# Feed-forward on Trainium2: four token tiles a group, weights kept once, and the x rows held until the output

## The reference

```python
x = x + _L0_attn_ref(_layernorm(x), ...)
x = x + 0.5 * _L0_ffn_ref(_layernorm(x), ...)   # top-2 of 8 experts, gelu(gate) * up, down
x = x + 0.5 * _L1_ffn_ref(_layernorm(x), ...)   # below
x = x + _L1_attn_ref(_layernorm(x), ...)
x = x + 0.5 * _L1_ffn_ref(_layernorm(x), ...)

def _L1_ffn_ref(x, gate_w, up_w, down_w, gate_s, up_s, down_s):
    g = jnp.einsum('th,ih->ti', xf, gate_w) * gate_s      # 512 -> 1408
    u = jnp.einsum('th,ih->ti', xf, up_w) * up_s
    hdn = jax.nn.silu(g) * u
    out = jnp.einsum('ti,hi->th', hdn, down_w) * down_s   # 1408 -> 512
```

## Time and profile before

| | |
|---|---|
| time, median of 3 runs | 4873.7 us (4868.59 to 4876.05) |
| span of the profiled execution | 4868.5 us; its own time is taken as the nearest of the runs, 4868.59 us |
| TensorE busy | 4669.5 us, 96% |
| VectorE, ScalarE, GpSimd busy | 60%, 46%, 48% |
| mean granted TensorE clock | 0.975 of full |
| transfers | 593.49 MB, mean 122 GB/s |

### The profile page before, as it was taken

The page is one execution under the profiler, slowest core; times in us unless marked ns, Lnnn a source line. Parts: engine busy times, 40 slices in busy tenths (PEclk is TensorE's granted clock), DMA queues, the critical chain, the costliest instruction groups (busy, mean ns, idle before and its releaser), DMA issues. The chain is left out here.

```text
span 4868.5 us, 89120 instructions
## 1 busy us (share of the span) xinstructions
PE 4669.5 (96%) x30652; PEld 3639.6 (75%) x30653; DVE 2927.7 (60%) x5637; ACT 2238.0 (46%) x4551; POOL 2328.8 (48%) x1768
## 2 busy tenths in 40 slices
PE   6999996999999999999998799999899999999999
PEld 4788885666666666666656588887899987689999
DVE  6222225789999999999965522222655548774444
ACT  4222223466666666666662322222544335453333
POOL 1545433178888888888880335451411116430000
PEclk8999998899999999999999899999999999999999
DMA  7233226657777777777765623332522322251110
GB/s 220 80 93 100 91 85 228 238 109 147 147 147 147 147 147 147 147 147 147 147 126 181 188 90 97 94 98 66 195 92 92 95 86 61 80 185 51 53 53 32
DMA packets 253209, 593.49 MB, mean 122 GB/s; under 512 B 31616, under 2 KB 85888, under 8 KB 228352
## 3 DMA queue, kind: packets, MB, share of 16 engines
q0 software_dynamic: 62064, 317.23, 29.0%
q1 hardware_dynamic: 190736, 271.21, 17.0%
HBM read 262.22 MB, written 121.11 MB: 79 GB/s over the span
## 5 line engine op out<-in xcount | busy, mean ns | idle before, releaser
L1464 POOL TENSOR_TENSOR attend_pairs<-attend_pt 128x1024 f32<-128x1024 f32 x512 | 1257.6, 2476 | 198.6 <-ACT attend_pt L1429 197.9
L1477 DVE TENSOR_REDUCE attend_mx<-attend_am_ps 128x1 f32<-128x512 f32 x2048 | 1251.8, 679 | 123.9 <-PE attend_am_ps L1337 120.6
L1429 ACT ACTIVATE attend_pt<-attend_sc_ps 128x512 f32<-128x512 f32 x2048 | 1039.9, 617 | 283.9 <-PE attend_sc_ps L1325 283.6
L1337 PE MATMUL attend_am_ps<-attention_kst,attend_qst 96*128 96x512 f32 x2048 | 859.3, 425 | 9.2 <-DMA attend_qst<-q_parts 9.1
L1325 PE MATMUL attend_sc_ps<-attend_qst,attention_kst 98*128 98x512 f32 x2048 | 816.3, 400 | 1.5 <-ACT attend_pt L1429 1.3
L1337 PEld LDWEIGHTS attend_am_ps<-attention_kst,attend_qst 96*128 96x128 f32 x2048 | 393.1, 192 | 239.7 <-DVE attend_mx L1477 123.0
L727 DVE TENSOR_TENSOR expert_ac<-expert_gu_ps,expert_gl 128x512 f32<-128x512 f32 x142 | 98.3, 692 | 666.9 <-ACT expert_gl L687 666.9
L1351 PE MATMUL attend_pv_ps<-attend_pt,attention_v 128*32 128x256 f32 x8192 | 493.6, 381 | 0.0
L1325 PEld LDWEIGHTS attend_sc_ps<-attend_qst,attention_kst 98*128 98x128 f32 x2048 | 389.8, 191 | 86.9 <-ACT attend_pt L1429 11.7
L1351 PEld LDWEIGHTS attend_pv_ps<-attend_pt,attention_v 128*32 128x32 f32 x8192 | 246.3, 110 | 211.5 <-ACT attend_pt L1429 45.9
L1832 ACT ACTIVATE ffn_sg<-ffn_gu_ps,ffn_gs 128x256 f32<-128x256 f32 x352 | 167.1, 475 | 506.9 <-PE ffn_gu_ps L1753 506.9
(11 more groups left out here) (347 smaller groups left out, 9114.9 us busy)
## 6 DMA issues: line engine op xcount, KB each, us to landing
attend_pairs<-attend_pairs POOLq DMA_DIRECT2D x189, 1024.0 KB, 7.4
weights_raw<-experts_dram POOLq DMA_DIRECT2D x76, 512.0 KB, 4.2
ys<-expert_ob SPq DMA_DIRECT2D x142, 256.0 KB, 2.3
attend_qst<-q_parts SPq DMA_DIRECT2D x192, 128.0 KB, 3.9
yn<-route_yb SPq DMA_DIRECT2D x64, 256.0 KB, 4.0
ffn_xb<-x SPq DMA_DIRECT2D x64, 256.0 KB, 2.8
ffn_rb<-x SPq DMA_DIRECT2D x64, 256.0 KB, 3.0
keyvalue_xb<-x SPq DMA_DIRECT2D x64, 256.0 KB, 2.8
```

The costliest lines, as they stand in the source:

```text
L1337: pe.matmul(am[:, bank, :], qst[0:KROWS, n % 2, h * HALF + hd, :], kst[0:KROWS, o:o + 4 * P], start=True, stop=True).then_inc(am_rdy, 1)
L1429: act.activation(pt[:, u % RING, g * 4 * P:(g + 1) * 4 * P], sc[:, s % SBANKS, :], ACT.Exp, scale=HD ** -0.5).then_inc(p_rdy, 1)
L1464: pool.tensor_tensor(pairs[:, slot(half, j), :], pt[:, 2 * p % RING, :], pt[:, (2 * p + 1) % RING, :], ALU.add).then_inc(pair_rdy, 1)
L1477: dve.tensor_reduce(mx[:, hh, block:block + 1], am[:, am_slot["max", a] % MBANKS, :], AX.X, ALU.max).then_inc(mx_rdy, 1)
```

## The change

- Groups of four tiles, with one of two tiles at either end: 9 groups in place of 16. Gate and up move 512 columns a matmul. The down projection stays as it was, tile by tile. `y_hi` and `y_lo` have one buffer in place of two; the next group's first two tiles are turned after the first tile's down projection, the other two in the middle of the second tile's.
- The weights are kept once: they are loaded straight into an fp32r buffer, with no split on any engine, and every group multiplies two products (`y_hi` and `y_lo` by the weight). If the flag says that low parts exist, the same operands are multiplied as plain float32 instead.
- The test moves into the second expert stage: in every second of its steps SyncE loads a piece of the weights and copies it to a scratch tensor in memory, ScalarE rounds the piece, VectorE compares and keeps the maximum. A reduction near the stage's end gives `low_seen`. ffn0 turns it into the flag at its very start; ffn1 uses the same flag.
- The x rows stay in `xb` (eight tiles) until the output; neither the joined x rows nor a second read of x goes through memory.
- In ffn0 all gathers are issued by GpSimd without casts between them. Statistics of the next group's tiles stand at blocks 1, 3, 5 and 7 of a group.

The diff, cut to its core:

```diff
 # expert_stage, only where tested
+                if tested and k == 0 and not last:                       # sync
+                    sp.wait_ge(ever_rdy, i + 1)
+                    sp.dma_start(raw_c[:], ffn_w[:, bass.ds(i, 1), :].rearrange("p a d -> p (a d)")).then_inc(c_in, 16)
+                    sp.dma_start(ffn_kept[:, bass.ds(i, 1), :], ffn_w[:, bass.ds(i, 1), :]).then_inc(c_kept, 16)
                 sp.wait_ge(ob_rdy, j + 1)
...
                     out(j - 1, k, i)                                      # scalar
+                    if tested and k == 0:
+                        act.wait_ge(c_in, i * 16 + 16)
+                        act.activation(hi_c[:], raw_c[:], ACT.Copy).then_inc(chi_rdy, 1)
...
                     x_part(j + 1, k)                                      # vector
+                    if tested and k == 1:
+                        dve.wait_ge(chi_rdy, i + 1)
+                        dve.tensor_tensor(differs[:], raw_c[:], hi_c[:].bitcast(F32), ALU.not_equal).then_inc(differs_rdy, 1)
+                        dve.wait_ge(differs_rdy, i + 1)
+                        dve.tensor_tensor(ever[:], ever[:], differs[:], ALU.max).then_inc(ever_rdy, 1)
 # ffn_stage
-GF = 2
+GF = 4
+FIRST = 2
+GROUPS = [(0, FIRST)] + [(t, GF) for t in range(FIRST, NT - GF + 1, GF)] + [(NT - FIRST, FIRST)]
...
+            def up(g, m, width, exact):
+                k = m % 2
+                pe.wait_ge(h_rdy, g * IC + max(m + 1, 2))
+                for q, done in enumerate((g_rdy, u_rdy)):
                     for c in range(DC):
+                        for n, y in enumerate((y_hi, y_lo)):
+                            a, b = w[:, 2 * m + q, c * P:(c + 1) * P], y[:, c, 0:width]
+                            if not exact:
+                                a, b = a.bitcast(F32), b.bitcast(F32)
+                            ins = pe.matmul(gu[:, k, q, 0:width], a, b, start=(c == 0 and n == 0), stop=(c == DC - 1 and n == 1))
+                    ins.then_inc(done, 1)
...
+            def step(g, first, n, following, exact):
+                pe.wait_ge(lo_rdy, first + n)
                 for m in range(IC):
+                    if isinstance(g, int) and g == 0:
+                        pe.wait_ge(gu_in[m], 16)
+                    up(g, m, n * P, exact)
+                after = [(first + n + j, (FIRST + j) % NY) for j in range(following)]
+                down(g, first, 0, exact)
+                for tile, slot in after[0:2]:
+                    turn(tile, slot)
+                down(g, first + 1, 1, exact, after[2:4])
+                for j in range(2, n):
+                    down(g, first + j, j, exact)
...
             warm(pe, const, tr[:, 0, 0:P], 50 if joined else 34)
+            if low_seen is not None:
+                pe.wait_ge(cmp_rdy, 1)
+                pe.matmul(gu[0:1, 1, 0, 0:1], const["ones"][:, 0:1], low_seen[:], start=True, stop=True).then_inc(cmp_rdy, 1)
+                pe.wait_ge(flag_rdy, 1)
...
+            if low_seen is not None:                                      # vector, ahead of stats(0)
+                dve.tensor_scalar(low_seen[:], low_seen[:], 0.0, None, ALU.not_equal).then_inc(cmp_rdy, 1)
+                dve.wait_ge(cmp_rdy, 2)
+                dve.tensor_scalar(flag[:], gu[0:1, 1, 0, 0:1], 1.0, None, ALU.min).then_inc(flag_rdy, 1)
+            for t in tiles(0):
+                stats(t)
+                moments(t)
+            for t in tiles(0):
+                scales([t])
+                normalise(t)
+            for t in tiles(0):
+                low(t)
...
+                for t in following:                                       # vector, at a group's end
+                    normalise(t)
+                for t in following[0:2]:
+                    low(t)
...
+                output(GROUPS[g][0])
+                for t in following[2:4]:
+                    low(t)
+                for t in list(tiles(g))[1:]:
+                    output(t)
```

More of the change, by code:

```diff
@@ L1671, in _, with tiles, columns, both @@
+        def tiles(g):
+            return range(GROUPS[g][0], sum(GROUPS[g])) if g < NG else range(0)
+        def columns(t):
+            at = t if t < FIRST else (t - FIRST) % GF
+            return slice(at * P, (at + 1) * P)
+        def both(part):
+            return slice(2 * part, 2 * part + 2)
         @block.sync
         def _(sp):
-            for t in range(GF):
-                f.load(sp, t, t)
+            def load(t):
+                sp.dma_start(xb[:, t % NX, :], x[bass.ds(t * P, P), :]).then_inc(x_in[t % NX], 16)
+            for t in range(FIRST):
+                load(t)
@@ L1756, in compare, with turn @@
-            def compare():
-                pe.wait_ge(diff_rdy, 2)
-                pe.wait_ge(h_rdy, IC + 1)
-                pe.matmul(gu[0:1, 1, 0, 0:1], const["ones"][:, 0:1], total[:], start=True, stop=True).then_inc(diff_rdy, 1)
-            def down(g, j, low, first=False):
-                pe.wait_ge(o_rdy, g * GF + (j + 1))
+            def turn(t, k):
+                pe.wait_ge(y_rdy, t + 1)
+                if not (isinstance(t, int) and t < 2):
+                    pe.wait_ge(lo_rdy, t - 1)
+                for c in range(DC):
+                    ins = pe.transpose(tr[:, k % 2, c * P:(c + 1) * P], yb[:, k, c * P:(c + 1) * P], const["ident"][:])
+                ins.then_inc(tr_rdy, 1)
@@ new lines, in step, with groups @@
+                after = [(first + n + j, (FIRST + j) % NY) for j in range(following)]
+                down(g, first, 0, exact)
+                for tile, slot in after[0:2]:
+                    turn(tile, slot)
+                down(g, first + 1, 1, exact, after[2:4])
+                for j in range(2, n):
+                    down(g, first + j, j, exact)
+            def groups(g0, g1, exact):
+                for g in range(g0, g1):
+                    step(g, *GROUPS[g], len(tiles(g + 1)), exact)
@@ L1873, in _ @@
+            for t in tiles(0):
+                high(t)
+            act.wait_ge(s_in, 32)
+            for g in range(NG):
                 for m in range(IC):
@@ L1976, in _ @@
+            dve.wait_ge(s_in, 32)
+            for g in range(NG):
+                following = list(tiles(g + 1))
                 for m in range(IC):
```

548 lines of the change are left out of this document (174 added, 374 removed).

## The result

The changed kernel took 4833.11 us (median of 4 runs, 4831.27 to 4834.08) against 4874.14 us before: a ratio of 0.9916, 95% interval 0.9902 to 0.9930. It is faster, by 41 us, not by the 61 that I forecast, and lies 3 us above the upper end of my range. The profiled execution spans 4829.6 us, 38.9 less than before.

A forecast was written before the change was run, and what follows sets the result against it. TensorE's stream was taken to set the time, other engines counting at starts and ends of stages. Terms of -31.1, -32.8, +0.6, +5.9, -2.5, -0.4 and +0.6 sum to -59.7, giving 4813 us (range 4804 to 4819).

The forecast's parts named there:

- Width: Gate and up in 14 groups of four: 512-column matmuls at 0.2266 us replace pairs at 0.120, -32.8 us.
- R1: Rival, gate and up: wide matmuls miss the steady spacing, 0.231 us, width gives 22 not 33, 4824 us; chance 0.15.
- Third product: First group of both feed-forward stages: a third of its matmuls goes, 15.6 us a stage, -31.1 us together.
- Start of ffn0: Start of ffn0: VectorE waits for the flag behind all 50 dummies, TensorE begins at about 3442.2, +5.9 us.
- clock and weights: First group of ffn0: waits for split weights go (-4.3), half clock after idling costs 1.8; -2.5 us.
- 1.8 + 0.6: First group of ffn0: 1.8 us allowed for half clock and 0.6 for waits on VectorE.
- R2: Rival: stalls between groups or more clock lost at ffn0's start; ten group changes at 1 us, 4823 us; chance 0.12.
- Start of ffn1: Start of ffn1: only the split of the first weight pieces falls away, TensorE starts at 4335.9, -0.4 us.
- Test in the expert stage: Second expert stage: test hidden in mid-stage, delays the chain in the tail, +0.6 us (0 to 2).
- R3: Rival, second expert stage: late test pieces hold TensorE at each of 34 pieces; 4915 us at 3 us each; chance 0.03.
- R4: Rival, feed-forward stages: flag comes out as 1, all products run as plain float32, near 7600 us; chance 0.01.

The follow-up runs named there:

- e13: The changed kernel with 320 unused bytes ahead of y, so that weights, y and h lie at distance 0 modulo 512 bytes: 4815.02 us, ratio 0.9885.
- e2: The changed kernel with all 16 groups of two tiles instead of groups of four, everything else kept: 4835.21 us, ratio 0.9927.
- e4: The changed kernel with the flag's matmul ahead of the 50 dummy matmuls of ffn0: 4828.38 us, ratio 0.9913.
- e9: e4 with SyncE's wait for the first gathered rows moved behind the second pair of weight pieces: 4833.64 us, ratio 0.9917.

## Why the prediction was wrong

*Width (-32.8): the step that failed.* I took 0.2266 us from down projections, and 0.120 for what it replaces, and carried both into a kernel in which y had been placed anew. In the layout of before both hold. In e13 the stages shrink by 28.15 us (554.01 to 525.86) and 32.5 (539.7 to 507.2), where the sum said 28.0 and 32.4. Part of that closeness is luck: in ffn0 the start cost 0.5 us less than my term and the first group 0.8 more, once its two additional turned tiles are set aside. So, in part, is the 4815 us for my 4813: by its ratio of 0.9885 e13 gains 55 us of the 60 that I forecast for the change. In the layout that the change really has, the wide form costs 6.7 ns more, 2464 x 6.7 ns = 16.5 us, down some 2 ns more (3 us), and the 704 narrow ones of the small groups up to 6 ns less (some -3). These 16 us cover the 15.4 by which the two stages fell short. So the term of -32.8 measured some -16 for the spacing of gate-and-up, and the reason was the place of the operands. R1 pointed this way with too small a price (0.231, 4824) and the wrong cause: I looked for a disturbance in time, and it was one in space.

What the width is worth depends on the layout. In ffn1, where TensorE waits for nothing in mid-stage, groups of four are 16.25 us shorter than groups of two at distance 0 (507.17 against 523.42, forecast 16.4), and not shorter at all at 192 (514.62 against 514.44). In ffn0 they are 22.0 shorter (525.86 against 547.86) and 6.2 (534.14 against 540.30). The 6 us more are not the width's spacing: there VectorE also joins and takes statistics, and a block of two tiles is too short to hide that. In the middle of ffn0 of e2 (3500 to 3900 us) the list of TensorE's waits has

```profile
PE ffn_gu_ps L1637 <- DVE ffn_hf L1774: 2.2, 12, 0.4
```

and its groups take 31.9 us, where those of ffn1 take 31.8 and 30.9 in turn; with groups of four the list is empty. The kernel before has 32.0 us a group in both stages, so these waits came with the rest of the change. By the ratios the width is worth 39 us at distance 0 and 5 at 192.

The Trainium skill ("TensorE: Matmul & The Clock Gate", section "Back-to-back issue gap") has, for matmuls by themselves, a gap that is nearly all columns, so that widening saves 2.5 ns a pair, 3 us a stage. At distance 0 the rows show 13.3 ns a matmul that do not grow with the columns (2 x 120.0 - 226.7); at distance 192 two narrow ones take 227.0 or 235.6 ns, by their rhythm, against 233.3 for a wide one, and ffn1 gains nothing. All of these spacings lie above the page's. The measurement decides: neither "2.5 ns" nor "13 ns" is true for every place of the operands.

*Third product (-31.1).* The amount is right (first groups -16.0 and -16.2 for 15.6 each), the reason incomplete: alone it is worth 7. I should have written it as product and preparation together.

*Start of ffn0 (+5.9) with clock and weights (-2.5).* The cause is right: VectorE's idle time ends with the flag's matmul. It measured +4.9 at the start, and the first group of ffn0 36.25 us against 32.0 in ffn1, so 4.2 for the 1.8 + 0.6 allowed: some 2.3 us of half clock (24 matmuls at 0.21 us), the rest in short pauses beside the next tiles' statistics and in the slower rhythm of the narrow form. That is the part of R2 that came. There is a term under it that I had not seen: e4 gains the start back and meets transfers at a share of 1.03.

*Start of ffn1 (-0.4).* Measured -0.5 (12.19 us after the stage's start against 12.67).

*Test in the expert stage (+0.6).* Hidden in mid-stage as argued, at 9.28 us a step: R3 is out. In the last step it costs 0.5, as forecast. The stage was 3.6 us longer in these two profiles, 3.0 in the means: 3.1 of the 3.6 stand before the first down projection, where the kernel before also varies from 23.0 to 27.4, and 0.8 to 1 us over the next 66 steps came with the change and stays open. R4 is out: at 0.2333 us apart gate and up are not plain float32.

*The rest of the 21 us* by which the span missed: 3.9 ahead of the change, +3.0 in the expert stage, -1.4 in keyvalue.

## What to carry to other kernels

A spacing that is read from a trace belongs to the addresses of its two operands as well as to its shape. When a change moves a small tensor ahead of a large one, measure again, and compare the starts modulo 256 bytes of what stands and what moves before you price a matmul, and set the distance with unused bytes: here 320 of them are worth 15 us by the ratios (0.9916 to 0.9885), 18 by the medians, and 192 of them 27 us in the kernel before (0.9945), for its narrow form. The same change of program is thus worth 56 us with distance 0 on both sides (1 to 0.9885) and only 14 with 192 on both (0.9945 to 0.9916): compare two kernels at the same distance before you credit a gain to anything else. Beyond that, a cost in a stage that two engines share (third product, low parts) is priced by what remains when it alone is gone, and not by its count.

## What the runs showed of the hardware

- The spacing of matmuls of gate-and-up and down, each with a weight load of its own, varied with the distance of standing to moving operand: 227.1 to 236.7 ns at 512 columns, 113.5 to 119.9 at 256, the same again after 256 bytes. The two widths don't go along: distance 0 is the best for 512 and nearly the worst for 256. Only 0 and 192 were tried in whole kernels.
- At 192 bytes the narrow form has two rhythms, 113.4 and 117.8 ns, and keeps one through 176 matmuls; a break may change it (in turn from group to group in ffn1 of e2).
- With the DMA share at 1.01, TensorE idled 5.4 us in seven places within a stream of dummies that waits for no semaphore (e9). The cause is not shown.
- VectorE operations of 0.69 us with both inputs in SBUF took up to 2.77 us where a GpSimd instruction that reads SBUF ran beside them (second expert stage of the kernel after, 14 of 68).
- After 5.71 us of idling, TensorE's granted clock was 0.50 from 3446 to 3453 us, and narrow matmuls stood 0.21 us apart in place of 0.1135.
